# An attention and feed-forward kernel: the chunk loops of PE, ACT and DVE written out as a straight program

## The reference

```python
q = x @ Wq.T + bq; k = x @ Wk.T + bk; v = x @ Wv.T + bv      # split into 16 heads of 16
q, k = rope(q), rope(k)
scores = softmax(q @ k.T / sqrt(256))                         # per head, 4096 x 4096
x = layernorm(x + (scores @ v) @ Wo.T)
h = silu((x @ w1.T) * s1) * ((x @ w2.T) * s2)
h = gelu((h @ h1.T) * sh1)
h = gelu((h @ h2.T) * sh2)
x = layernorm(x + (h @ w3.T) * s3)
```

## Time and profile before

| what | us |
|---|---|
| median of 3 runs | 3811.35 (3811.04 to 3815.56) |
| the profiled execution, its own time | 3821.48 |
| its span, first to last instruction | 3819.9 |
| PE, DVE, ACT marked busy | 3526.6, 2932.8, 2462.1 |

### The profile page before, as it was taken

How to read it: one execution, slowest core, us unless ns; L and a number is a source line. 1 busy time by engine, 2 the same in 40 slices (tenths; PEclk the granted TensorE clock), 3 DMA queues, 4 the chain that set the end, 5 groups by cost and what they waited for, 6 DMA issues and landing times. The chain is left out here.

```text
span 3819.9 us, 63480 instructions
## 1 busy us (share of the span) xinstructions
PE 3526.6 (92%) x20130; PEld 1516.0 (40%) x20130; DVE 2932.8 (77%) x3148; ACT 2462.1 (64%) x4472; POOL 196.4 (5%) x352
## 2 busy tenths in 40 slices
PE   8569999999999999999999999999998869999999
PEld 3223333333333333332333333333332158888887
DVE  6698999899899989998998999899983035555554
ACT  2118888788888878888887888788886512222222
POOL 3200000000000000000000000000000011111100
PEclk9759999999999999999999999999997589999999
DMA  8940000000000000000000000000000051111100
GB/s 208 212 137 12 12 12 12 13 12 12 23 12 12 12 13 12 12 12 17 18 12 13 12 12 12 12 12 23 8 8 4 3 182 35 34 34 44 40 17 12
DMA packets 64516, 125.61 MB, mean 33 GB/s; under 512 B 12551, under 2 KB 24904, under 8 KB 63032
## 3 DMA queue, kind: packets, MB, share of 16 engines
q1 hardware_dynamic: 59528, 114.02, 10.6%
q0 software_dynamic: 4704, 7.81, 0.7%
HBM read 90.59 MB, written 41.16 MB: 34 GB/s over the span
## 5 line engine op out<-in xcount | busy, mean ns | idle before, releaser
L646 DVE TENSOR_REDUCE group_max<-wide 128x2 f32<-128x1024 f32 x2048 | 2406.0, 1219 | 277.9 <-PE wide L507 277.6
L624 ACT ACTIVATE probs<-scores 128x512 f32<-128x512 f32 x4096 | 2223.3, 595 | 524.6 <-PE scores L572 431.5
L572 PE MATMUL scores<-q_sb,k_all 51*128 51x512 f32 x4096 | 1053.5, 511 | 148.6 <-ACT probs L624 62.7
L532 PE MATMUL sums<-probs,v_all 128*17 128x512 f32 x8192 | 1117.7, 619 | 0.0
L572 PEld LDWEIGHTS scores<-q_sb,k_all 51*128 51x128 f32 x4096 | 391.7, 188 | 1384.3 <-ACT probs L624 1355.7
L507 PE MATMUL wide<-k_all,q_sb 48*128 48x512 f32 x4096 | 807.3, 459 | 76.3 <-DVE group_max L646 50.2
L507 PEld LDWEIGHTS wide<-k_all,q_sb 48*128 48x128 f32 x4096 | 397.9, 191 | 394.8 <-DVE group_max L646 363.8
L1029 ACT ACTIVATE whole_hid<-acc,scale 128x512 f32<-128x512 f32 x128 | 84.6, 688 | 346.8 <-PE acc L910 346.7
L910 PE MATMUL acc<-hid_b,h2T 128*128 128x512 f32 x1024 | 241.6, 397 | 0.0
L910 PE MATMUL acc<-hid_a,h1T 128*128 128x512 f32 x1024 | 240.2, 395 | 0.0
L532 PEld LDWEIGHTS sums<-probs,v_all 128*17 128x17 f32 x8192 | 137.4, 96 | 258.2 <-ACT probs L624 150.7
(11 more groups left out here) (77 smaller groups left out, 1156.9 us busy)
## 6 DMA issues: line engine op xcount, KB each, us to landing
k_all<-k_parts SPq DMA_DIRECT2D x96, 128.0 KB, 5.0
q_sb<-q_parts SPq DMA_DIRECT2D x192, 64.0 KB, 2.3
w_words<-ff_weights SPq DMA_DIRECT2D x32, 352.0 KB, 3.1
q_parts<-parts SPq DMA_DIRECT2D x16, 512.0 KB, 5.6
k_parts<-parts SPq DMA_DIRECT2D x16, 512.0 KB, 6.2
heads<-mixed SPq DMA_DIRECT2D x32, 256.0 KB, 2.5
heads_sb<-heads SPq DMA_DIRECT2D x8, 1024.0 KB, 4.9
shares<-shares_dram POOLq DMA_DIRECT2D x112, 64.0 KB, 2.3
```

What stands on the lines that cost most here:

```text
L532: last = pe.matmul(sums[32 * j:32 * j + HD + 1, :], v_all[:, g, kt, j], probs[(kt * HG + j) % RING][:], start=(kt == 0), stop=(kt == KT - 1))
L572: pe.matmul(scores[(s + e) % BANKS][:], k_all[rows, g * GP + j, kt * P:(kt + 1) * P], q_sb[g][rows, j], start=True, stop=True).then_inc(sc ...
L624: act.activation(probs[n % RING][:], scores[s % BANKS][:], ACT.Exp, scale=INV_SCALE)\
L646: dve.reduce_max(group_max[:, n], wide[n % 2][:], AX_X).then_inc(wide_free, 1)
```

## The change

Five loops of the hardware become plain Python loops, so that the program of the engine is written out with constants: PE's and ACT's loop over chunks in attention, and PE's, ACT's and DVE's in the feed-forward net. No matrix multiplication, activation or transfer is added, removed or moved. The loops of DVE, POOL and SP in attention stay, and those of POOL and SP in the net.

```diff
@@ attend, PE
-            with pe.Fori(0, NCH - 1) as c:
+            for c in range(NCH - 1):
                 for g in range(1, NG):
                     unit(c, g)
                 unit(c + 1, 0)
@@ attend, ACT
-            with act.Fori(0, NCH - 1) as c:
+            for c in range(NCH - 1):
                 for g in range(1, NG):
                     unit(c, g)
                 unit(c + 1, 0)
@@ feed_forward, PE
-                with pe.Fori(0, NCH // 2 - 1) as half:
+                for half in range(NCH // 2 - 1):
                     for p in range(2):
                         step(half * 2 + p, p)
                 step(NCH - 2, 0)
@@ feed_forward, ACT
-            with act.Fori(0, NCH // 2 - 1) as half:
+            for half in range(NCH // 2 - 1):
                 for p in range(2):
                     step(half * 2 + p, p)
             step(NCH - 2, 0)
@@ feed_forward, DVE
-            with dve.Fori(0, NCH // 2 - 1) as half:
+            for half in range(NCH // 2 - 1):
                 for p in range(2):
                     step(half * 2 + p, p)
             step(NCH - 2, 0, more=False)
```

## The result

The changed kernel takes 3838.52 us in the median of four runs (3832.09 to 3841.64), the kernel before 3811.68 (3811.04 to 3815.56): a ratio of 1.0066, 95% interval 1.0049 to 1.0084. It is slower, as forecast, and by 26.8 us where 15.6 were predicted. Five later runs, next to fifteen of the kernel before on one chip, gave 3839.83 against 3816.68, 1.0052 (1.0039 to 1.0066). The profiled executions stand at spans of 3830.5 and 3819.9, 10.6 us apart.

A forecast was written before the change was run, and what follows sets the result against it. Attention was taken as bound by a ring PE, ACT, PE, with PE and DVE nearly full, the net by PE. Waits +44.5, back-edges -28.9 and net 0 give +15.6 on 3811.35: 3827 us, range 3813 to 3839.

The forecast's parts named there:

- The back-edges: Attention, units 1 to 28: six taken loop branches, each a gap plus one to two slow steps, vanish; -28.9 us.
- The waits: ACT in attention, units 1 to 28: the late wait becomes its own instruction, 0.06 us per step; +44.5 us.
- The sum: Units 1 to 28 of attention: waits and back-edges together, 2401.84 against 2386.21 us; +15.6 us.
- rival 5: Straight attention steps: the granted clock falls to 1.2 GHz for a while; ten such steps +14 us, 3841; 6%.
- The net: Feed-forward net: branches and added waits stay hidden behind PE's work, chunks stay 90.0 us; 0 us.
- 1: Attention, units 1 to 28: the waits cost nothing, so the kernel is faster by 28.9 us, 3782; 8%.
- rival 2: Attention: extra wait smaller without the profiler, 0.025 to 0.041 us per step; -7 to +7 us, 3804 to 3819; 11%.
- 4: Attention: straight code also waits for its instructions, once per former iteration, so stalls stay; +44.5 us, 3856; 6%.
- The profile against the other runs: Whole kernel before: the profiled execution's own time, 3821.48 us, is 10.1 us or 0.27% above the median of 3811.35.

The follow-up runs named there:

- straight_swapped: The changed kernel with the two waits of ACT's first activation of a step in the other order (scored, then probs_free): 3768.24 us, 0.9868 of the kernel before.
- loops_swapped: The kernel before, all loops kept, with the two waits of ACT's first activation of a step in the other order: 3859.98 us, 1.0117.
- after_again: The changed kernel run again without alteration: 3839.83 us.
- act_only: The kernel before with only ACT's attention loop written out: 3866.68 us, 1.0132.
- after_warm: The changed kernel with extra wide matmuls on PE, results unread, in steps of units 30 and 31 without wide groups: 3788.78 us.
- third_wait: The changed kernel with a third, long satisfied wait (sums_free) at ACT's first activation of a step: 3831.91 us, 1.0036 of the kernel before.
- the warm kernels: The kernel before and the changed kernel, each with unread wide matmuls on PE in steps of units 30 and 31 without wide groups: 3769.92 and 3788.78 us.
- net_only: The kernel before with only the three loops of the feed-forward net written out: 3816.40 us against 3816.68, 0.9996.
- pe_only: The kernel before with only PE's attention loop written out: 3806.89 us, 0.9973.

## Why the prediction was right, and where its size was off

The sign and both mechanisms were right. That the median fell into the range was a near thing: 3838.52 lies 0.5 us below its upper end of 3839, two of the four runs and the later median of 3839.83 above it. Of the 11.5 us over the 3827 that was forecast, 3.4 are mis-sized terms and 8 are not in its sum at all.

- *The back-edges, -28.9 us.* Right: straight_swapped, in which the waits cost nothing, gains 30.6 us in units 1 to 28. The two pairs of units that the prediction shows, 5.9 and 5.5 us over plain ones, are among the dearest; the other four cost 3.7 to 5.6 us by the trace of before, and the six sum to 29. The Trainium skill's rule in "Runtime: NRT & Kernel Launch", section Instruction fetch mechanics, agrees with the six branches of 3.4 to 4.0 us and with this gain; it did not give the sign of the change, which the waits decided.
- *The waits, +44.5 us.* The mechanism is shown in both directions (straight_swapped, loops_swapped); the size was too small, it is 49.6. The forecast took 85.78 us for a straight unit from unit 29, the only full one outside the loops at clock 1.00. In the changed kernel the 28 units are 85.90 in the mean: the step has a median of 2.658, where it is 2.656 in unit 29 of the kernel before, and six steps take 2.93 to 2.95 us. One of them is in the rows below; all six come at the same steps in after_again, act_only, after_warm and third_wait, and none is in straight_swapped. And the plain unit to compare with is 84.13 (2355.63 / 28), not 84.19.

```profile
742.98 2.26 ACT L624 ACTIVATE probs<-scores 128x512 f32<-128x512 f32 x4 [0.39 <-PE scores L572]
745.91 2.27 ACT L624 ACTIVATE probs<-scores 128x512 f32<-128x512 f32 x4 [0.67 <-PE scores L572]
```

- *The sum, +15.6 us.* +19.0 in the profile, +18.9 between the warm kernels. The rest of the +26.8 of the first comparison, 8 us, does not show between the warm kernels: the kernel before had a median of 3811.68 in the first four runs and of 3816 to 3817 in 38 later ones, on three chips (that of the first runs is not on record), and the end of attention alone moves a profile by up to 10 us. Which of these made the 8 us is not settled. The prediction named the fall of the clock after the wide groups, but only as a danger to straight units (rival 5); that the same fall blurs the comparison itself it did not see.
- *The net, 0.* Right: net_only, 0.9996. That the branches there are always hidden is not: pe_only has one of 3.8 us that cost 1.6 us of a chunk. The prediction read only branches of 0.22 and 0.25 us.
- *Rivals.* 1 and 2 (cheap or half-priced waits) are out by 49.6 us, or 0.055 per step where 0.032 decides. 4 (straight code stalls too) is out, but for the six steps of 0.27 us. 5 (the clock falls in straight units) is out: 1.00 throughout units 1 to 28.
- *The profile against the other runs.* The 10.1 us between profile and median, which rival 2 leaned on, need no cost of profiling: later runs of the kernel before go up to 3822, and the profiled executions of net_only (3813.39) and third_wait (3823.82) lie below the medians of their kernels.

## To carry to other kernels

Before loops are written out, look at each instruction with two waits on the ring that sets the pace. In these traces the first wait stated stays on the instruction in the straight form and the others go to one ahead of it; in the loop form it is the last one that stays. State the late wait where it lands on the instruction itself; here that was worth 49.6 us, more than all branches. And look for a stretch where the granted clock falls at a moment that differs from run to run, here 8 to 47 us after the wide groups end: once PE was given matmuls there, the comparison of two kernels got sharper, not only the kernels faster.

## What was not expected of the hardware

- A wait on an instruction of its own is free if it is satisfied early (1024 of them in straight_swapped) and costs 0.06 us a step if it is the late one; with two waits in one such instruction it is 0.05 (a median step of 2.646 in third_wait, against 2.597).
- Matmuls that nobody reads made unit 31 faster by 45 us (129.07 to 84.11), and the granted clock there was 1.00 and not 0.50.
- Six steps of 2.93 to 2.95 us at fixed places. Counted among ACT's instructions in the trace of the changed kernel, the late waits of the first five are 256 or 512 apart, and every late wait at a place of that spacing is slow; the sixth is 2688 further on, ten and a half times 256. A page has 256 instructions by the Trainium skill ("Runtime: NRT & Kernel Launch", section Instruction fetch mechanics). That the late wait meets the end of such a page is argued, not shown: the spacing fits five of the six, and no run here moved them.
- PE's branch back over four units took 3.4 to 4.0 us, by the trace of the kernel before (median in the earlier trace rows). Over two chunks of the net it took 0.22 to 0.25, but 3.8 us once in pe_only, whose program of the net is the same; why there is not known.
